# The second norm's token shift by a transfer, new orders on all engines, and the final additions spread over the drain

## The reference, cut to what matters

```
x = attn_layer(shift_tokens(x), Wqkv, q_scale, k_scale, Wo) + x      # 16 heads of 64, windows of 32 tokens
x = ffn_layer(shift_tokens(x), ln_g, ln_b, W1, b1, W2, b2) + x       # layernorm, gated gelu, W2
def shift_tokens(t):                # the second half of the features comes from the token before
    a, s = jnp.split(t, 2, -1)
    s = jnp.pad(s, ((0, 0), (1, 0), (0, 0)))[:, :-1]
    return jnp.concatenate([a, s], -1)
```

## Time and profile before

| what | value |
|---|---|
| median of 3 runs | 3379.66 us (3376.93 to 3380.09) |
| the profiled execution | 3372.05 us, span 3370.2 us |
| busy PE, DVE, ACT, POOL | 97%, 85%, 82%, 74% of the span |
| granted TensorE clock, mean | 0.991 of full speed |

### The profile page before, as it was taken

One profiled execution on the slowest core, in us unless ns is written; L12 is line 12 of the kernel. 1 busy time (PEld: TensorE's weight loads), 2 busy tenths in 40 slices (PEclk: granted clock), 3 DMA queues, 4 the chain that ended last, 5 costly groups with the idle time before them and its releaser, 6 DMA issues.

```text
span 3370.2 us, 170013 instructions
## 1 busy us (share of the span) xinstructions
PE 3264.7 (97%) x65892; PEld 2345.6 (70%) x65892; DVE 2873.8 (85%) x6037; ACT 2751.3 (82%) x5265; POOL 2505.5 (74%) x2703
## 2 busy tenths in 40 slices
PE   6998799999999999999999999999999999999997
PEld 3444477777777777777777777777777777777775
DVE  5888788888888888888888888888888888888885
ACT  3666788888888888888888888888888888888886
POOL 3554677777787777778777787877777787777773
PEclk9999999999999999999999999999999999999998
DMA  2000121112212122221212212122211112221212
GB/s 77 8 7 5 39 57 47 53 50 67 69 47 56 47 55 68 61 55 47 56 47 75 61 49 54 47 56 67 68 48 51 52 47 79 57 56 47 53 50 55
DMA packets 125541, 175.94 MB, mean 52 GB/s; under 512 B 26742, under 2 KB 49332, under 8 KB 124724
## 3 DMA queue, kind: packets, MB, share of 16 engines
q1 hardware_dynamic: 125492, 175.28, 19.4%
HBM read 21.32 MB, written 2.10 MB: 7 GB/s over the span
## 4 chain that ended last, share of the span: by engine, by line
PE 78%; POOL 10%; issue 7%; DMA 1%; DVE 1%; ACT 1%; SPq 1%; POOLq 0%; ACTq 0%; DVEq 0%
PE bank L1149 16%; PE bank L1259 9%; PE bank L1167 9%; PE bank L1159 8%; PE bank L1230 7%; PE bank L1214 6%; POOL qk L452 4%; POOL qk L461 4%; PE bank L1051 3%; PE bank L1293 3%; PE bank L1247 3%; PE bank L1301 3%; PE bank L1268 2%; PE bank L1206 2%; POOL P L490 1%
## 5 line engine op out<-in xcount | busy, mean ns | idle before, releaser
L452 POOL TENSOR_TENSOR qk<-ta,tb 128x512 f32<-128x512 f32 x768 | 982.6, 1280 | 13.0 <-DVE tb L872 13.0
L1149 PE MATMUL bank<-wqkv,zsT 128*128 128x512 f32 x1536 | 806.6, 607 | 6.9 <-ACT zsT L659 2.6
L461 POOL TENSOR_TENSOR qk<-qk,rn 128x512 f32<-128x512 f32 x768 | 795.6, 1048 | 0.0
L610 ACT ACTIVATE sq<-bank 128x512 f32<-128x512 f32 x768 | 461.1, 600 | 322.6 <-PE bank L1149 313.5
L490 POOL TENSOR_TENSOR P<-P,rowsum 128x512 f32<-128x512 f32 x384 | 401.3, 1045 | 375.2 <-DVE rowsum L988 375.2
L869 DVE TENSOR_TENSOR ta<-bank,rot 128x512 f32<-128x512 f32 x768 | 525.8, 685 | 26.7 <-ACT sq L610 11.4
L872 DVE TENSOR_TENSOR tb<-bank,rot 128x512 f32<-128x512 f32 x768 | 521.2, 679 | 0.0
L973 DVE TENSOR_REDUCE bank<-sq 128x32 f32<-128x2048 f32 x192 | 437.8, 2280 | 0.3
L1159 PE MATMUL bank<-wqkv,zsT 128*128 128x512 f32 x768 | 412.3, 619 | 5.4 <-DVE tb L872 5.4
L1259 PE MATMUL bank<-wo,oT 128*128 128x128 f32 x3072 | 393.9, 281 | 0.7 <-ACT oT L636 0.7
L1259 PEld LDWEIGHTS bank<-wo,oT 128*128 128x128 f32 x3072 | 357.3, 191 | 13.8 <-ACT oT L636 1.1
(11 more groups left out here) (133 smaller groups left out, 6298.3 us busy)
## 6 DMA issues: line engine op xcount, KB each, us to landing
vs<-vt SPq DMA_DIRECT2D x1152, 128.0 KB, 2.4
wqkv<-L_ffn_Wqkv SPq DMA_DIRECT2D x6, 1024.0 KB, 5.1
wqkv<-L_ffn_Wqkv SPq DMA_DIRECT2D x6, 512.0 KB, 3.8
wo<-L_ffn_Wo SPq DMA_DIRECT2D x6, 512.0 KB, 3.7
z_sb<-x SPq DMA_DIRECT2D x4, 512.0 KB, 6.9
ctxb<-ctx SPq DMA_DIRECT2D x32, 64.0 KB, 1.7
out<-x_sb SPq DMA_DIRECT2D x8, 256.0 KB, 3.5
w<-L_ffn_W SPq DMA_DIRECT2D x6, 341.0 KB, 3.1
```

Of the source, the lines that this page charges most:

```text
L452: g.tensor_tensor(o, i0, i1, ALU.add).then_inc(s["g_add"], 1)
L461: g.tensor_tensor(q3, q3, r3, ALU.mult).then_inc(s["g_qk"], 1)
L610: a_.activation(sq[:, 512 * j:512 * j + 512], bank[j % 2][:, :], ACT.Square)\
L1149: t_.matmul(bank[j % 2][:, :], zsT[:, k % 2, :], wqkv[:, 512 * j:512 * j + 512], start=True, stop=True).then_inc(s["p_qk"], 1)
```

## The change: what it does

- `zm` gets three parts of 64 features: first half, shifted second half, second half. `z_mid` writes parts 0 and 2. A transfer on SP, `shift_z`, copies part 2 of tokens 0 to 126 to part 1 of tokens 1 to 127; part 1 of token 0 is zeroed once at the start. PE's `shift_tokens` goes. `norm_stats` waits for the transfer, and `norm_stats` and `norm_apply` read parts 0 and 1 of `zm` in SBUF and no longer bank 6. `residual` reads parts 0 and 2.
- `shift_z` of unit u stands ahead of `shift_v` of unit u+3 on SP; at the end of a layer they stand between the loads, and `shift_z` of the first unit of a layer is behind `load_ffn`.
- `sum_rows` and `invert` move from the end of slot n to the start of slot n+1 on DVE (lag 3).
- PE, ACT, DVE and POOL get new orders. `attend` now waits for the values itself, where `values_here` did.
- The final additions are in nine pieces, eight of them at the ends of DVE's slots 192 to 195, where their sequences are ready, and one of a single sequence behind the last slot. SP stores them as they come.

The diff, cut to its core:

```diff
-        zm = sb("zm", [128, 2, E])
+        zm = sb("zm", [128, 2, 3, E // 2])
...
+        OUT_AT = {UNITS: ((0, 4), (4, 8), (8, 12)), UNITS + 1: ((12, 16), (16, 20), (20, 24)),
+                  UNITS + 2: ((24, 28),), UNITS + 3: ((28, 31),), UNITS + 4: ((31, 32),)}
...
+            def shift_z(u, par):
+                wait(sp, "d_zm", count(1, u, 1))
+                sp.dma_start(zm[1:128, par, 1, :], zm[0:127, par, 2, :]).then_inc(s[f"l_s{par}"], 16)
...
                 with sp.Fori(0, (B - 6) // 2) as i:
                     for k in range(2):
+                        shift_z(i * 2 + (start + k), k)
                         shift_v(i * 2 + (start + 3 + k), (3 + k) % 2)
...
+                if layer + 1 == DEPTH:
+                    store(0, 6)
+                shift_z(end - 1, 1)
+                if layer + 1 < DEPTH:
                     shift_v(end + 2, 0)
                     load_ffn(layer + 1)
-            for c in range(8):
-                sp.wait_ge(s["d_out"], c + 1)
-                sp.dma_start(ov[:, 4 * c:4 * c + 4, :], x1v[:, 4 * c:4 * c + 4, :]).then_inc(s["out_done"], 16)
-            sp.wait_ge(s["out_done"], 128)
+            store(6, 9)
+            sp.wait_ge(s["out_done"], 144)
...
# POOL
+                next_input()
+                add(0)
                 norm_rstd()
+                normalize(0)
                 residual()
-                add(0)
-                normalize(0)
                 normalize(1)
                 add(1)
+                add(2)
                 normalize(2)
-                next_input()
                 normalize(3)
-                add(2)
                 weigh(0)
+                weigh(1)
                 add(3)
-                weigh(1)
# ACT
                 square(0)
                 copy_T(0)
+                copy_T(1)
+                square(1)
                 log_sum()
-                copy_T(1)
                 inverse_root()
-                square(1)
                 copy_T(2)
                 copy_T(3)
                 square(2)
-                act.preload_act_table_set("gelu_and_others")
                 copy_z()
                 copy_PT(0)
+                copy_PT(1)
+                square(3)
+                act.preload_act_table_set("gelu_and_others")
                 copy_zn()
-                square(3)
-                copy_PT(1)
+                copy_o(0)
+                copy_o(1)
                 copy_v(0)
                 gelu()
                 act.preload_act_table_set("natural_log_exp_and_others")
                 exponent()
-                copy_o(0)
-                copy_o(1)
                 copy_v(1)
# DVE
-                        wait(dve, "p_zsh", count(1, d - 2, 1))
-                        v_.tensor_tensor(zm[:, pd, :], bank[7][:, 384:512], z_sb[:, cols(d)], ALU.add)\
+                        v_.tensor_tensor(zm[:, pd, 0:3:2, :], bank[7][:, 384:512].rearrange("p (c e) -> p c e", c=2),
+                                         z_sb[:, cols(d)].rearrange("p (c e) -> p c e", c=2), ALU.add)\
...
-                        wait(dve, "p_zsh", count(1, d, 1))
-                        v_.bn_stats(stats[:, 0:6], bank[6][:, 0:128]).then_inc(s["d_bn"], 1)
+                        wait(dve, f"l_s{pd}", 16 * (d // 2) + 16 if isinstance(d, int) else (d >> 1) * 16 + 16)
+                        v_.bn_stats(stats[:, 0:6], zm[:, pd, 0:2, :].rearrange("p c e -> p (c e)"))\
...
-                        v_.tensor_scalar(zn[:, :], bank[6][:, 0:128], mv[:, 0:1], rstd[:, pd:pd + 1],
+                        v_.tensor_scalar(zn[:, :], zm[:, pd, 0:2, :].rearrange("p c e -> p (c e)"), mv[:, 0:1], rstd[:, pd:pd + 1],
...
+                root(0)
+                sum_rows()
+                z_mid()
+                invert()
+                rotary(0)
+                rotary(1)
+                root(1)
+                root(2)
+                root(3)
+                rotary(2)
+                norm_stats()
+                norm_aggr()
+                norm_var()
                 z_out()
-                root(0)
-                z_mid()
-                rotary(0)
-                root(1)
-                norm_stats()
-                root(2)
-                norm_aggr()
-                root(3)
-                norm_var()
-                rotary(1)
+                maximum(0)
                 norm_apply()
-                rotary(2)
-                maximum(0)
+                rotary(3)
                 maximum(1)
                 subtract(0)
-                rotary(3)
                 subtract(1)
+                sum_squares()
                 gated()
-                sum_squares()
-                sum_rows()
-                invert()
+                if isinstance(n, int) and UNITS <= n < UNITS + 4:
+                    output(OUT_AT[n])
# PE
                 proj_qk(0)
-                ffn_out()
                 transpose_qk(0)
                 attn_out()
                 proj_qk(1)
                 transpose_qk(1)
-                shift_tokens()
+                ffn_out()
                 proj_qk(2)
                 transpose_z()
+                proj_qk(3)
                 transpose_P()
                 scores()
+                attend()
                 transpose_zn()
-                proj_qk(3)
-                values_here()
                 proj_v(0)
                 ffn_gate()
+                proj_v(1)
                 ffn_a()
-                attend()
-                proj_v(1)
```

More of the change, by code:

```diff
@@ L92, in build @@
         ident = cst[:, C_ID:C_ID + 128]
-        shift = cst[:, C_SH:C_SH + 128]
         tri = cst[:, C_TRI:C_TRI + 128]
@@ L340, in _, with store @@
                     load_ffn(0)
+            sp.wait_ge(s["u_s0"], 1)
+            ov = out.rearrange("b s e -> s b e")
+            def store(first, last):
+                for c in range(first, last):
+                    lo, hi = OUT_PARTS[c]
+                    sp.wait_ge(s["d_out"], c + 1)
+                    sp.dma_start(ov[:, lo:hi, :], x1v[:, lo:hi, :]).then_inc(s["out_done"], 16)
             for layer in range(DEPTH):
@@ L348, in _ @@
                     for k in range(2):
+                        shift_z(i * 2 + (start + k), k)
                         shift_v(i * 2 + (start + 3 + k), (3 + k) % 2)
+                shift_z(end - 6, 0)
                 shift_v(end - 3, 1)
+                shift_z(end - 5, 1)
                 if layer + 1 < DEPTH:
@@ L355, in _ @@
                     load_v(layer + 1)
+                shift_z(end - 4, 0)
                 shift_v(end - 1, 1)
+                shift_z(end - 3, 1)
                 if layer + 1 < DEPTH:
                     shift_v(end, 0)
+                shift_z(end - 2, 0)
+                if layer + 1 < DEPTH:
                     shift_v(end + 1, 1)
                     load_o(layer + 1)
+                if layer + 1 == DEPTH:
+                    store(0, 6)
+                shift_z(end - 1, 1)
+                if layer + 1 < DEPTH:
                     shift_v(end + 2, 0)
                     load_ffn(layer + 1)
-            ov = out.rearrange("b s e -> s b e")
-            for c in range(8):
-                sp.wait_ge(s["d_out"], c + 1)
-                sp.dma_start(ov[:, 4 * c:4 * c + 4, :], x1v[:, 4 * c:4 * c + 4, :]).then_inc(s["out_done"], 16)
-            sp.wait_ge(s["out_done"], 128)
+            store(6, 9)
+            sp.wait_ge(s["out_done"], 144)
         @block.gpsimd
@@ L1021, in _, with output @@
+            def output(parts):
+                for lo, hi in parts:
+                    dve.wait_ge(s["z_ready"], B + UNITS - (B - hi))
+                    dve.wait_ge(s["x_store"], B)
+                    cc = slice(E * lo, E * hi)
+                    v_.tensor_tensor(x1_sb[:, cc], x1_sb[:, cc], z_sb[:, cc], ALU.add).then_inc(s["d_out"], 1)
+            slots(dve, slot)
+            output(OUT_AT[UNITS + 4])
         @block.tensor
@@ L1234, in attend @@
                                 ins.then_inc(s["p_AV"], 1)
-                def values_here():
-                    if c_on:
-                        wait(pe, f"l_v{pc}", 96 * (c // 2) + 96 if isinstance(c, int) else (c >> 1) * 96 + 96)
                 def ffn_out():
@@ L1255, in attn_out @@
                         wait(pe, "l_wo", 16 * layer_of(d) + 16)
-                        edge(pe, n, "a_gelu", count(1, d - 1, 1))
+                        wait(pe, "a_gelu", count(1, d - 1, 1))
                         edge(pe, n, "a_zs", count(2, zu - 1, 2))
@@ L1261, in attn_out @@
                         ins.then_inc(s["p_y"], 1)
-                def shift_tokens():
-                    if d_on:
-                        wait(pe, "d_zm", count(1, d, 1))
-                        wait(pe, "z_ready", (count(1, f, 1) if isinstance(f, int) else d) + B)
-                        t_.matmul(bank[6][:, 0:64], ident, zm[:, pd, 0:64], start=True, stop=True)
-                        t_.matmul(bank[6][:, 64:128], shift, zm[:, pd, 64:128], start=True, stop=True)\
```

(1 more changed line is left out.)

35 lines of the change are left out of this document (19 added, 16 removed).

## The result

The changed kernel takes 3352.61 us (five runs, 3345.50 to 3355.75) against 3379.66; the ratio is 0.992 (95% interval 0.9907 to 0.9932). The forecast was 3286 with a range of 3238 to 3350. The direction was right; -27 us instead of -94, and the time is just outside the range. The profiled execution took 3345.50 (span 3343.7) against 3372.05 (span 3370.2): -26.5 us of span to explain.

What follows compares the result with a forecast made beforehand. PE was taken to bound the loop: -0.53 us x 187 slots = -99, +11 at layer ends, -3 for start, drain and tail: -91, so 3281 profiled, 3289 as median; stated 3286, range 3238 to 3350.

Steps and rivals of the forecast that it cites:

- What bounds the kernel: Main loop: PE never waits in its 15.45 us slot, so removed PE work shortens it until another engine binds.
- PE's list, 14.92: PE's work per slot: matmuls removed and pieces reordered, -0.53 us in sum, for a slot of 14.92 (14.58 to 15.30).
- Position of `z_mid` ... No wait: Within a slot: the second rotary ends at 6.67, PE reaches `proj_qk(3)` at 6.82, so PE does not wait.
- if PE shows waits for `rotary`: Sign on PE's timeline that the forecast is wrong, named with waits for `copy_zn`; no size given.
- `norm_apply`, 0 to +0.70, took +0.1: DVE's `norm_apply`, now SBUF to SBUF: may block with POOL, costing 0 to +0.70 us; +0.1 taken.
- a ring binds: Rival, steady slot: blocked `norm_apply` or late `exponent` gives slots of 15.1 to 15.3, about 3335 us; chance 0.17.
- The transfer: Shift transfer on SP: D = 4.2 us if one engine takes all rows, hidden up to D = 5.3.
- the line: Shift transfer's packets: a line from 4 bytes to 2 KB gives 21.5 ns for 256 bytes.
- Layer ends: Five layer ends: `shift_z` queued behind `load_ffn` loses 2.6 us each; net +11 us (0 to +20).
- Start, drain and tail: Outside the full loop: start 0, drain +3.5, tail -6.3 us; together -3.
- The chance of 0.56: Probability given to the forecast itself, 3262 to 3312 us.
- the sum gave 3289: Whole kernel: -91 us from the profiled 3372.05 gives 3281; the runs' median, 7.6 above, gives 3289; 3286 was stated.

Runs made afterwards that it cites:

- e13: e5 with GpSimd's `residual` moved ahead of `normalize(0)`, and `normalize(0)` made to wait until `norm_apply` is done; 3276.08 us, ratio 0.9711.
- e7: The changed kernel's new orders with the shift still on PE, behind `ffn_out`, the norm read from bank 6, no transfer; 3353.71 us, ratio 0.9933.
- e5: The changed kernel with the transfer in two parts, `rotary(0)` ahead of `z_mid`, and `shift_z` ahead of `w1` at layer ends; 3361.44 us, ratio 0.996.
- e14: The changed kernel with `rotary(0)` ahead of `z_mid` and `residual` ahead of `normalize(0)`, the transfer whole; 3337.20 us, ratio 0.9884.

## Why the prediction was wrong, step by step

- **What bounds the kernel: right.** PE's list is the bound as long as nobody makes it wait.
- **PE's list, 14.92: right.** 14.93 once the waits are gone (e13). In that kernel's chain `ffn_out` takes 0.86 and both projections 0.86, as forecast. Three smaller terms were off and cancelled by luck: the gate takes 0.79 instead of 0.66, `attend` behind the scores 1.55 instead of 1.63, `transpose_zn` 0.26 instead of 0.31.
- **"Position of `z_mid` ... No wait": the step that failed.** It compared the end of the second rotary, 6.67, with the end of the piece that PE has in front of `proj_qk(3)`, 6.82, and called the 0.15 between them slack. In the short slots both came out as forecast, 6.66 and 6.82, and the projection still costs 0.16 more than its 0.86. PE's weight load wants the bank 0.27 before the piece in front has ended (e13), at 6.55, and the handoff takes 0.06; the sum had neither. In the long slots `z_mid` starts 0.39 after `attn_out` ends, not 0.22 as in the short ones (0.24 before). DVE's queue has four register instructions between the two in each of the 88 long slots that I counted and two in each of the 88 short ones, as the two bodies of the unrolled loop alternate; they are the likely reason, not a tested one. That puts `z_mid` at 3.88 instead of 3.72 and the second rotary's end at 6.87. Now `proj_qk(2)` waits too, for `rotary(0)`, which I had not looked at: the two take 1.00 and 1.09 in the chain. Price: 0.16 and 0.37 in turn, 0.26 per slot, half of the gain (e7 and e13 show it from both sides). The prediction's own sign of being wrong, "if PE shows waits for `rotary`", is the one that came.
- **`norm_apply`, 0 to +0.70, took +0.1: right for this kernel, where it took 0.34,** by the luck of its place. It is the next bound, as soon as the rotary is early: e5 with 15.39 and e13 with 14.93 differ by the collision and the two edits on GpSimd that avoid it. The rival "a ring binds" (3335) thus named the right bottleneck for e5. The changed kernel's own slots of 15.19 are in its range of 15.1 to 15.3, by another wait.
- **The transfer: right.** D was 3.70 against 4.2, one engine, hidden in every steady slot (e14). A packet of 256 bytes took 18.8 ns, against the 21.5 of the line.
- **Layer ends: mechanism right, size wrong,** +17.5 instead of +11. Counted as in the forecast, `gated` ends at 2.6 in the slot instead of 2.0, so the issue is at 8.4 and not 7.8; PE pauses 2.84 to 3.33 instead of 2.6, and the lower clock adds some 1.6 at four of the five.
- **Start, drain and tail: the drain mis-sized,** +10.6 in its slots instead of +3.5. I had costed one slot of it, and no change of order in it. The tail gave -4.6 instead of -6.3.
- **The chance of 0.56 for a slot with 0.15 to 0.40 us of slack beside three other engines was too high.** The handoff to `z_mid` alone, 0.24 before and 0.22 or 0.39 now, is as large as that slack. And the sum gave 3289; the 3286 has no working.

## What to carry to other kernels

When work leaves the bounding engine, the other engines' results must be early by that much too: check each wait in the list against its own producer, take the time at which the waiting engine's first instruction (for PE the weight load) wants the result, and count slack of the size of the handoffs (0.2 to 0.4 us here) as none. A `tensor_scalar` from SBUF to SBUF on VectorE belongs where GpSimd is surely between instructions; if both queues are full, make GpSimd wait. In a queue, put the short transfer that someone waits for ahead of the loads that nobody needs yet, and give a transfer a number of partitions that divides well.

## What the runs showed of the hardware that I had not expected

- Slots can alternate in length, for two reasons here. 14.80 (three times) and 15.80, or 14.57 and 15.80, come from a collision: between two of them `z_mid` runs ahead of PE's 14.92. 15.12 and 15.26 go with the two bodies of the unrolled loop, as do the 15.14 and 15.61 of e7, where PE's own distance is 15.37 each time. The shortest of such slots is no engine's steady time; the mean is what counts.
